# Adding the constant of the squared queries inside two VectorE products instead of in a GpSimd pass, in an unrolled linear-attention and FFN kernel

## The reference

```
gate = sigmoid(x @ W_gate + b_gate);  gate = gate / (mean(gate) + EPS)
q = relu(q * gate) ** 2 + EPS          # EPS = 1e-5
k = relu(k * gate) ** 2 + EPS
kv_s += k_t (x) v_t;  k_s += k_t       # running sums over the sequence, per head
num = q_t . kv_s;  den = (q_t . k_s) + EPS
out = (num / den) @ W_proj + b_proj
```

## Time and profile before

| | |
|---|---|
| median of 3 runs | 1857.77 us |
| the profiled execution's own time | 1856.67 us |
| its span, first to last instruction | 1854.6 us |
| PE busy | 1805.0 us (97%) |
| DVE busy | 1415.2 us (76%) |
| POOL busy | 880.9 us (48%) |
| ACT busy | 683.6 us (37%) |
| granted TensorE clock, mean | 0.994 |
| queries + EPS on POOL (L386) | 79.9 us, 64 instructions |

### The profile page before, as it was taken

The page is one execution under the profiler, slowest core; times in us unless marked ns, Lnnn a source line. Parts: engine busy times, 40 slices in busy tenths (PEclk is TensorE's granted clock), DMA queues, the critical chain, the costliest instruction groups (busy, mean ns, idle before and its releaser), DMA issues.

```text
span 1854.6 us, 34416 instructions
## 1 busy us (share of the span) xinstructions
PE 1805.0 (97%) x13753; PEld 1541.8 (83%) x13753; DVE 1415.2 (76%) x2606; ACT 683.6 (37%) x1242; POOL 880.9 (48%) x1091
## 2 busy tenths in 40 slices
PE   6899999999999999999999999999999999999997
PEld 3688888888888888888888888888888888888876
DVE  6777777777777777777777777777777777777775
ACT  4233333333433433433433433433333333333332
POOL 3345545545545545545545544545454445455440
PEclk9999999999999999999999999999999999999999
DMA  5101010011010011010010010010100110100000
GB/s 193 41 18 35 24 36 24 24 35 35 24 35 24 24 35 35 24 35 24 24 35 28 32 33 21 28 35 24 35 24 26 33 35 24 36 24 24 29 19 23
DMA packets 34509, 61.07 MB, mean 33 GB/s; under 512 B 3672, under 2 KB 6256, under 8 KB 34352
## 3 DMA queue, kind: packets, MB, share of 16 engines
q1 hardware_dynamic: 33488, 57.31, 9.4%
q10 hardware_dynamic: 864, 1.57, 0.3%
HBM read 41.96 MB, written 16.91 MB: 32 GB/s over the span
## 4 chain that ended last, share of the span: by engine, by line
PE 73%; POOL 14%; ACT 5%; DVE 2%; issue 1%
PE ps_a L768 8%; PE ps_a L766 8%; PE ps_a L767 8%; POOL h_lo L366 6%; PE ps_b L768 6%; PE ps_b L767 6%; PE ps_b L766 6%; PE ps_t L773 5%; PE ps_q L766 4%; PE ps_q L767 2%; PE ps_q L768 2%; POOL key_lo L395 2%; ACT L450 2%; POOL xs L355 2%; POOL queries L386 2%; PE ps_h L766 2%
## 5 line engine op out<-in xcount | busy, mean ns | idle before, releaser
L366 POOL TENSOR_TENSOR h_lo<-h_full,h_hi 128x512 fp32r<-128x512 f32 x244 | 314.1, 1287 | 349.7 <-DVE h_hi L596 349.7
L450 ACT ACTIVATE h_full<-ps_h,cols 128x256 f32<-128x256 f32 x512 | 211.0, 472 | 242.5 <-PE ps_h L768 234.9
L596 DVE CAST h_hi<-h_full 128x512 fp32r<-128x512 f32 x256 | 163.4, 638 | 98.5 <-ACT h_full L450 98.4
L328 POOL TENSOR_TENSOR small<-moments,eps_col 128x1 f32<-128x1 f32 x128 | 25.8, 202 | 393.9 <-DVE moments L735 325.7
L766 PE MATMUL ps_a<-wx_hi,zt_hi 128*128 128x512 f32 x512 | 207.9, 406 | 0.0
L766 PE MATMUL ps_b<-wx_hi,zt_hi 128*128 128x512 f32 x512 | 206.4, 403 | 1.2 <-DVE key_sums L698 0.9
L768 PE MATMUL ps_b<-wx_hi,zt_lo 128*128 128x512 f32 x512 | 203.1, 397 | 0.0
L767 PE MATMUL ps_b<-wx_lo,zt_hi 128*128 128x512 f32 x512 | 203.1, 397 | 0.0
L768 PE MATMUL ps_a<-wx_hi,zt_lo 128*128 128x512 f32 x512 | 202.4, 395 | 0.0
L767 PE MATMUL ps_a<-wx_lo,zt_hi 128*128 128x512 f32 x512 | 201.9, 394 | 0.0
L766 PE MATMUL ps_q<-h_hi,u_hi 128*128 128x256 f32 x512 | 162.7, 318 | 15.5 <-POOL h_lo L366 9.2
(11 more groups left out here) (160 smaller groups left out, 5133.1 us busy)
## 6 DMA issues: line engine op xcount, KB each, us to landing
xs<-L_attn_x SPq DMA_DIRECT2D x64, 256.0 KB, 2.7
out<-x1s SPq DMA_DIRECT2D x64, 256.0 KB, 2.1
key_sums<-carry_rows SPq DMA_DIRECT2D x60, 256.0 KB, 3.2
x1s<-L_attn_W_qkv SPq DMA_DIRECT2D x8, 256.0 KB, 5.1
x1s<-L_attn_W_gate SPq DMA_DIRECT2D x4, 256.0 KB, 4.0
h_full<-L_attn_W_qkv SPq DMA_DIRECT2D x4, 256.0 KB, 6.4
x1s<-L_ffn_U SPq DMA_DIRECT2D x4, 256.0 KB, 3.6
carry_rows<-key_sums SPq DMA_DIRECT2D x64, 2.0 KB
```

The lines of the kernel that those rows point to most:

```text
L366: E.tensor_tensor(h_lo[:, i % 2, :], h_full[:, i % 2, :], h_hi[:, i % 2, :].bitcast(F32), ALU.subtract).then_inc(s["h_lo_ready"], 1)
L450: last = E.activation(h_full[:, i % 2, a * GROUP:(a + 1) * GROUP], ps_h[i % 2][:, a * GROUP:(a + 1) * GROUP], ACT.Gelu_apprx_tanh, bias=b1 ...
L596: E.tensor_copy(h_hi[:, i % 2, :], h_full[:, i % 2, :]).then_inc(s["h_hi_ready"], 1)
```

## The change

EPS is no longer added to the queries by GpSimd. Both VectorE instructions that read the queries afterwards add it themselves, with a scalar constant: the product with the key sums, and the division by the denominator. Both turn from `tensor_tensor` into `scalar_tensor_tensor`; their count stays. The first of them waits for VectorE's own third instruction of `squared_relu` instead of for GpSimd. The semaphore query_ready is gone. The keys are left as they are.

```
@@ gpsimd, step
                     pool.wait_ge(s["key_steps"], n.done(3, 3))
                     E.tensor_tensor(keys[:, n.half, :], keys[:, n.half, :], eps_wide, ALU.add)\
                         .then_inc(s["key_ready"], 1)
-                    pool.wait_ge(s["query_steps"], n.done(3, 3))
-                    E.tensor_tensor(queries[:, :], queries[:, :], eps_wide, ALU.add)\
-                        .then_inc(s["query_ready"], 1)
@@ vector, step
                     dve.wait_ge(den_steps, n.done(6, 1))
-                    dve.wait_ge(s["query_ready"], n.done())
-                    E.tensor_tensor(gate[:, :], key_sums[:, :], queries[:, :], ALU.mult).then_inc(den_steps, 1)
+                    dve.wait_ge(s["query_steps"], n.done(3, 3))
+                    E.scalar_tensor_tensor(out=gate[:, :], in0=queries[:, :], scalar=EPS, in1=key_sums[:, :],
+                                           op0=ALU.add, op1=ALU.mult).then_inc(den_steps, 1)
...
                     by_head = queries[:, :].rearrange("p (h d) -> p h d", d=HEAD)
-                    E.tensor_tensor(by_head, by_head, den[:, 2, :].unsqueeze(2).broadcast_to([P, NH, HEAD]),
-                                    ALU.mult).then_inc(den_steps, 1)
+                    E.scalar_tensor_tensor(out=by_head, in0=by_head, scalar=EPS,
+                                           in1=den[:, 2, :].unsqueeze(2).broadcast_to([P, NH, HEAD]),
+                                           op0=ALU.add, op1=ALU.mult).then_inc(den_steps, 1)
```

More of the change, by code:

```diff
@@ L193, in block_kernel @@
             key_done key_steps key_ready key_hi_ready key_lo_ready
-            query_done query_steps query_ready value_done value_ready
+            query_done query_steps value_done value_ready
             sums_done den_steps tk_done key_t_ready tq_done query_t_ready
```

## The result

The changed kernel takes 1838.16 us (median of 4 runs, 1837.18 to 1840.32) against 1856.26 (4 runs); the ratio is 0.9906, with a 95% interval of 0.9887 to 0.9925. Forecast were 1840.5 us, in a range of 1836 to 1852. The profiled execution took 1837.18 us, where the sum made against the profiled execution of before said 1840.0.

What follows compares the result with a forecast made beforehand. PE, busy 97%, was taken to bound the kernel, waiting for POOL's h_lo in even steps. 29 x 0.52 = 15.1, plus 0.8 and 0.8 at the start, gave 16.7 us and 1840.5 us, range 1836 to 1852.

Steps and rivals of the forecast that it cites:

- PE's lateness sets the gain: Third q_pair of even steps: PE's wait for POOL's h_lo costs 0.42 + 0.10 = 0.52 us, all of which goes.
- POOL's chain without the link: Even steps: without the pass the last h_lo ends at 927.58 instead of 928.16, in time for PE by 0.04 us.
- first rival: Even steps: key_lo takes 1.46 us, PE's wait stays in part, gain 0.26 per even step, 1848.5 us; chance 0.20.
- The odd steps give nothing: Odd steps: the pass lies in a hole where POOL idles 3.05 us for the first cast, so gain 0.
- VectorE's two instructions at 0: L705 and L715 in their new form cost 0 more; upper bound +0.25 us each.
- The sign that the product with the key sums keeps its length: A listed sign of being right: L705, VectorE's product with the key sums, keeps its length, mean 941 ns.
- slower rival: Dearer VectorE instructions delay x1t_lo in every even step; at +0.44 us (L705 at 1.13) 24 us lost, 1864.5; chance 0.05.
- What is late next: nothing: Even steps, gate's sigmoid and x1t_lo before the key transposes: no new PE wait, 0 us; the sigmoid fits by 0.02.
- 2d - 0.05: Key transposes of even steps: PE's longer wait for x1t_lo if each of VectorE's two instructions takes d more.
- Start, 0.8 + 0.8: First step's wait for key_lo gives 0.8 us (bounds 0 and 1.2); the longer wait at 145 us gives 0.8.
- The end, 0: The kernel's tail has no queries, so the forecast counted no gain there.
- the four cases: Chances: whole wait gone 0.62, in part 0.20, given back 0.13 (a third still counts as faster), slower 0.05.

Runs made afterwards that it cites:

- e2: The changed kernel with a spare GpSimd pass of 128 columns where the queries' pass was: 1843.21 us, ratio 0.993 to the kernel before.
- e5: The kernel before with the change made in odd steps alone, even steps keeping GpSimd's pass and the plain products: 1856.09 us, ratio 0.9996.
- e7: The kernel before, GpSimd's pass kept, with VectorE's two products turned into scalar_tensor_tensor adding a constant 0.0: 1855.96 us, ratio 0.9997.
- e9: The changed kernel with the constant added by a VectorE instruction of its own and plain products: 1850.51 us, ratio 0.9968 to the kernel before.
- e1: The changed kernel with a spare GpSimd pass of 512 columns where the queries' pass was: 1856.55 us, ratio 1.0004 to the kernel before.
- e10: The changed kernel with GpSimd's add_bias moved behind the h_lo of the third pair: 1837.02 us, ratio 0.9891 to the kernel before.

## Why the prediction was right

- **PE's lateness sets the gain.** Right: 0.42 + 0.10 us per even step were read and both went; the period fell by 0.55, where 0.52 was said. Aligned matmul by matmul, and averaged over 28 periods, 0.42 and 0.11 come at the two starts of rows 4; the last 0.02 are spread over the other starts, about 0.01 at most at each.
- **POOL's chain without the link.** Right to 0.03 us: counted from the third cast, the last `h_lo` was to end 2.64 us later and did 2.67 later; the second `h_lo` loses the rest of the link to its cast (0.36 us idle); the cast took 1.30 us and ended 0.27 after `key_lo`. `key_lo` took 1.30 us, near the 1.26 to 1.29 taken and not the 1.46 of the first rival. The real margin was 0.06 us: `h_lo` ended at 918.47, and the load came at 918.53. e2 shows how near the first rival was: 0.14 us more and the refill was back. It also shows that the rival was priced too high, at 0.26 us: in e2 a load 0.12 us late cost 0.14 in all, since the matmul ahead covers 0.12.
- **The odd steps give nothing.** Right, by e5.
- **VectorE's two instructions at 0.** Right for the form, by e7, and for the division (693 ns). The sign that the product with the key sums keeps its length failed: 0.79 became 1.28 us in even steps. The slower rival named 1.13 us as the mean from which 24 us are lost; the mean is 1.158, and nothing is lost. It had counted from 692, where 941 was the mean already, and all of the rise is in even steps, while the chain to `x1t_lo` begins in the odd ones. That the rise fell there was not foreseen.
- **What is late next: nothing.** Right in the outcome. The gate fits as narrowly as was said: its evacuation ends at 928.68, the table load at 928.66, and the sigmoid starts at 928.72. The place for the slower rival is real, by e9, but 2d - 0.05 is not its price: the 0.05 us are no slack, a late load is covered for 0.23 us by the matmul ahead, and 0.06 are lost behind the first transpose. That makes 0.48 - 0.23 + 0.06 = 0.31, where 0.33 were measured.
- **Start, 0.8 + 0.8.** The sum fits better than its terms. 1.8 us were measured from the first gate evacuation to the one behind the wait at 145 us, as VectorE sees it. Aligned matmul by matmul, PE is 1.5 us ahead just before that wait, where 0.8 had been taken and 1.2 was the upper bound, and 2.1 behind it, so the wait itself gave 0.5 as the others do, not 0.8. PE waits 2.4 instead of 3.6 us for `key_lo` in the first step, so 1.2 of the 1.5 are this term, at its upper bound; the other 0.3 I did not trace.
- **The end, 0.** Measured 2.0. Some 0.55 of it is the last even step's wait, whose effect VectorE sees only behind the bound of that stretch. The other 1.4 go together with the granted clock, 0.98 against 0.94 of 2.4 GHz in that stretch; no run shows that the clock is the cause of all of it. e1, which has the passes back, ends in 78.7 us, and the 14 profiles lie between 77.3 and 79.7 with and without the pass; so I don't count it to the change.
- **Sum.** 16.7 us forecast; 18.1 by the medians, 19.5 by the two spans. Of these, 1.5 + 0.5 + 29 x 0.55 = 18.0 us lie in the terms of the sum. The forecast median is 2.3 us off, and its errors point nearly all one way: each term but that of the wait at 145 us was too small. In the chances, the four cases add up to 0.86 for faster (0.62 + 0.20 + a third of 0.13), where 0.84 was written; nothing hangs on it.

## What to carry to other kernels

Work taken off a half-idle engine is worth what it takes off the chain that ends in a late instruction of the bounding engine, not its length: here 1.2 us per step gave 0.55 in every other step and nothing in the rest, and moving the same pass, or a neighbour, by one place gave the same or more. Read the bounding engine's lateness from the distances between its starts; idle time showed 0.26 of 0.52 us. And before counting further gains, look for the next instruction that starts the moment its operand is there, and for what covers it: a load that was just in time took 0.06 of the 0.23 us of e10. An operand that ends 0.05 us ahead of its reader is not early; compare the gap with one where the reader is known to wait.

## What was not expected of the hardware

A late weight load has two prices. Its own matmul is late only by what the matmul ahead does not cover: nothing for 0.12 us behind 256 columns (e2) or 0.23 behind 512 (e10), 0.25 for 0.48 behind 512 (e9). The start after that one is late on top, by 0.10 to 0.11 us between matmuls of 256 columns and by 0.06 between the transposes, even where the first was on time.

A longer instruction can cost nothing more, or even free another: with a pass of 256 columns instead of 128 ahead in GpSimd's order, the cast took 0.43 instead of 1.44 us, and the period was 55.51 us in both.

In the end stretch the granted clock was 0.94 of 2.4 GHz in one execution and 0.98 in another, in both behind a stretch in which PE waits for VectorE's `zs`; with 27.8 to 32.1 us for the start, most of the difference between profiled executions with the same period lies in the two ends; the periods of kernels with the same waits repeat to 0.03 us.
